# Folding rows h and -h ahead of the transform along h, and that transform in four 64x64 tiles of TensorE

## What is computed

```python
def afno_filter(x, w1, b1, w2, b2):
    xf = jnp.fft.rfft2(x, axes=(1, 2), norm='ortho')
    xf = xf.reshape(B, H, W // 2 + 1, NUM_BLOCKS, bs)
    xr, xi = (jnp.real(xf), jnp.imag(xf))
    o1r = relu(einsum(xr, w1[0]) - einsum(xi, w1[1]) + b1[0])
    o1i = relu(einsum(xi, w1[0]) + einsum(xr, w1[1]) + b1[1])
    o2r = einsum(o1r, w2[0]) - einsum(o1i, w2[1]) + b2[0]
    o2i = einsum(o1i, w2[0]) + einsum(o1r, w2[1]) + b2[1]
    yf = softshrink(o2r, LAM) + 1j * softshrink(o2i, LAM)
    return jnp.fft.irfft2(yf, s=(H, W), axes=(1, 2), norm='ortho') + x

h = layer_norm(x, n1_g, n1_b)
h = afno_filter(h, w1, b1, w2, b2) + x
residual = h
h = layer_norm(h, n2_g, n2_b)
h = gelu(h @ mw1 + mb1)
return h @ mw2 + mb2 + residual
```

## Time and profile before

| | us |
|---|---|
| median of 3 runs | 1629.3 (1629.04 to 1630.48) |
| the profiled execution, its own time | 1629.48 |
| its span, first to last instruction | 1627.7 |
| TensorE matmul busy | 1556.1 (96%) |
| VectorE busy | 990.3 (61%) |
| ScalarE busy | 889.3 (55%) |
| GpSimd busy | 620.4 (38%) |
| granted TensorE clock, mean | 1.000 |

### The profile page before, as it was taken

How to read it: one execution, slowest core, us unless ns; L and a number is a source line. 1 busy time by engine, 2 the same in 40 slices (tenths; PEclk the granted TensorE clock), 3 DMA queues, 4 the chain that set the end, 5 groups by cost and what they waited for, 6 DMA issues and landing times.

```text
span 1627.7 us, 43919 instructions
## 1 busy us (share of the span) xinstructions
PE 1556.1 (96%) x16132; PEld 1379.1 (85%) x16132; DVE 990.3 (61%) x2433; ACT 889.3 (55%) x1638; POOL 620.4 (38%) x782
## 2 busy tenths in 40 slices
PE   0999999999999899999999989999999989999999
PEld 0987888888998788888898888888889879888888
DVE  7967556656537665665655766565663675555553
ACT  5544366666534356666643436666662443666665
POOL 5800046776800017677660003667673000111111
PEclk9999999999999999999999999999999999999999
DMA  8410713333300062333420052333331006011111
GB/s 225 172 45 3 241 49 107 104 99 119 98 15 3 9 240 86 108 101 99 124 79 2 3 203 66 104 110 97 104 111 46 3 3 207 27 39 32 32 39 46
DMA packets 168583, 138.30 MB, mean 85 GB/s; under 512 B 10882, under 2 KB 132484, under 8 KB 168452
## 3 DMA queue, kind: packets, MB, share of 16 engines
q1 hardware_dynamic: 167268, 136.24, 26.6%
q10 hardware_dynamic: 1184, 0.20, 0.1%
HBM read 69.30 MB, written 67.11 MB: 84 GB/s over the span
## 4 chain that ended last, share of the span: by engine, by line
PE 93%; DVE 3%; ACT 1%; SPq 1%; DMA 1%; issue 1%; POOL 0%; ACTq 0%; DVEq 0%
PE ps L797 27%; PE ps L591 8%; PE ps L611 8%; PE ps L581 7%; PE ps L763 7%; PE ps L765 7%; PE ps L724 7%; PE ps L764 7%; PE ps L757 3%; PE ps L649 3%; PE ps L743 3%; PE ps L749 3%; SPq L431 1%; DMA first<-in_x_dram 1%; PE ps L779 1%
## 5 line engine op out<-in xcount | busy, mean ns | idle before, releaser
L797 PEld LDWEIGHTS ps<-mw,gel 128*128 128x128 f32 x4000 | 520.6, 191 | 42.3
L797 PE MATMUL ps<-mw,gel 128*128 128x128 f32 x4000 | 523.7, 274 | 0.0
L907 ACT ACTIVATE gel<-ps,mb1f 128x512 f32<-128x512 f32 x500 | 343.7, 687 | 250.6 <-PE ps L765 219.7
L1473 POOL TENSOR_TENSOR arena<-arena,mb2rep 128x512 f32<-128x512 f32 x125 | 160.2, 1282 | 634.5 <-ACT hn L893 634.5
L763 PE MATMUL ps<-hth,mw1h 128*128 128x512 f32 x512 | 259.7, 507 | 4.5 <-DVE vsb L1119 1.7
L1462 POOL TENSOR_SCALAR arena<-xnext,rstd,shift 128x128 f32<-128x128 f32 x360 | 159.4, 462 | 207.6 <-DVE shift L1356 207.6
L893 ACT ACTIVATE hn<-arena,shift,rstd 128x128 f32 (+1 forms) x512 | 221.6, 483 | 16.8 <-DVE shift L1356 16.8
L765 PE MATMUL ps<-hth,mw1l 128*128 128x512 f32 x512 | 202.1, 395 | 0.0
L764 PE MATMUL ps<-htl,mw1h 128*128 128x512 f32 x512 | 200.8, 392 | 0.0
L1203 DVE TENSOR_TENSOR arena<-ps,arena 128x512 f32 (+1 forms) x60 | 41.5, 691 | 252.0 <-PE ps L749 233.4
L871 ACT COPY gsb<-ps 128x512 f32<-128x512 f32 x128 | 69.1, 589 | 159.1 <-PE ps L611 153.0
(11 more groups left out here) (111 smaller groups left out, 2125.6 us busy)
## 6 DMA issues: line engine op xcount, KB each, us to landing
arena<-aside SPq DMA_DIRECT2D x128, 256.0 KB, 4.8
aside<-gz SPq DMA_DIRECT2D x96, 256.0 KB, 3.0
between<-xout SPq DMA_DIRECT2D x62, 256.0 KB, 2.3
out_dram<-xout SPq DMA_DIRECT2D x62, 256.0 KB, 2.3
xnext<-between SPq DMA_DIRECT2D x60, 256.0 KB, 3.0
aside<-first SPq DMA_DIRECT2D x32, 256.0 KB, 2.3
xnext<-in_x_dram SPq DMA_DIRECT2D x30, 256.0 KB, 3.1
first<-in_x_dram SPq DMA_DIRECT2D x1, 960.0 KB, 7.4
```

What stands on the lines that cost most here:

```text
L797: mm = pe.matmul(ps[:, r % 2, P * i:P * i + P], gel[:, r % 2, m, P * i:P * i + P], mw2[:, s // IMAGES, m, :], start=(m == 0 and i == 0), s ...
L907: act.activation(gel[:, r % 2, m, :], ps[:, 2 + m % 2], ACT.Gelu, bias=mb1f[:, s // IMAGES, m:m + 1]).then_inc(gelu_out, 1)
L1473: pool.tensor_tensor(t, t, b, ALU.add).then_inc(mb2_done, 1)
```

## The change

In steps 1 to 3 the rows of the image are laid out so that slots 64 to 127 hold the mirror rows (-h) of slots 0 to 63 in the same order (`zplace`; GpSimd and VectorE write the four rows of such a tile reversed).

dft_w becomes `mirrored`: each channel is done twice with 64 of the 128 slots as stationary operand, rows h into the even bank of a pair (sign 0) and rows -h into the odd bank (sign 1). Two channels, 64 partitions of output each, go to the two column halves of the array. A pair of banks (d, 16 of them) holds eight channels. ScalarE copies the bank of rows h to SBUF (`upper_copy`, into `hn`), then VectorE adds and subtracts the other bank (`fold_out`, two 128x512 operations) into the "folded" layout. TensorE waits for the folds of two pairs before (`evicted(s, 2 * d - 3)`).

dft_h then has 64 rows per product: sums with the even part (65 columns), differences with the sines and a correction (95 columns), for two halves of the array's rows. With both q together (`units=(0, 1)`) these are four 64x64 products on four different tiles. The two units of a pair are issued together, behind one wait for the copies of both, and signal together; units 0 and 1 at the start are issued singly, on two tiles. The frequencies along h are stored in another order (0, 64, evens, odds), with the same widths of the pieces in mix1 (65 and 63 columns). ih and idft_w take the lower half of the rows in the new order; `h2_odds` and `h2` read the reversed side on the subtraction instead of the addition. Step 0 stays as it was (`whole_dft_h`). The constants grow by 160 columns.

```diff
-CONSTS = 7 * P + MASKS
 EVEN = KWS + 1
+FOLD_E, FOLD_O = EVEN, P - EVEN + KWS // 2
+MASK_AT = 7 * P + FOLD_E + FOLD_O
+CONSTS = MASK_AT + MASKS
...
-    k_of = np.concatenate([k, -k[1:-1]])
+    ks = np.concatenate([[0, KWS], np.arange(2, KWS, 2), np.arange(1, KWS, 2)])
+    fh = np.concatenate([np.cos(turn * np.outer(h, ks)), np.sin(turn * np.outer(h, ks[2:]))], 1) * scale
+    k_of = np.concatenate([ks, -ks[2:]])
+    fold_e, fold_o = fh[:HALF, :EVEN].copy(), fh[:HALF, P - FOLD_O:].copy()
+    fold_e[-1] = scale * (ks % 2 == 0)
+    fold_o[:, :KWS // 2] = 0
+    fold_o[-1] = -scale * (np.arange(FOLD_O) < KWS // 2)
+    folds = np.tile(np.concatenate([fold_e, fold_o], 1), (2, 1))
     ih = np.concatenate([np.cos(turn * np.outer(k_of, h[:HALF + 1])),
                          np.sin(turn * np.outer(k_of, -h[HALF + 1:]))], 1) * scale
+    ih[:, HALF:] = ih[:, :HALF - 1:-1].copy()
     de = 2 * np.stack([cos, -sin], 2)[:, :KWS]
...
+        folded = [a.rearrange("p (k o a b d) -> p k o a b d", o=2, a=2, b=2, d=QUART) for a in flat]
...
+        def zplace(j, r):
+            return (2 * j + r // 2 + TILES // 2) * ROWS if r % 2 else tile_of(j, r) * ROWS
...
                 if s == 0:
                     pe.wait_ge(a_act, cg + 1)
-                elif cg % 2:
-                    pe.wait_ge(a_dve, CGROUPS // 2 * (s - 1) + cg // 2 + 1)
-                else:
-                    pe.wait_ge(a_act, CGROUPS + CGROUPS // 2 * (s - 1) + cg // 2 + 1)
+                else:
+                    pe.wait_ge(a_dve, CGROUPS * (s - 1) + cg + 1)
...
                 for cg in range(CGROUPS):
-                    if s and cg == 3:
-                        pe.wait_ge(lo_out, TILES * s)
+                    if s:
+                        mirrored(s, cg // 2, cg % 2)
+                        continue
                     if cg >= 4:
...
-            def dft_h(s, n):
+            def mirrored(s, d, sign):
+                if d == 1 and sign:
+                    pe.wait_ge(lo_out, TILES * s)
+                if d >= 2 and not sign:
+                    evicted(s, 2 * d - 3)
+                q, slots = d // 8, slice(HALF, H) if sign else slice(0, HALF)
+                for i in range(GROUP):
+                    for g in range(2):
+                        t = KWS // 2 * q + KWS // 4 * g + GROUP // 2 * (d % 8) + i // 2
+                        mm = pe.matmul(ps[HALF * g:HALF * g + HALF, 2 + 2 * (d % 2) + sign, P * i:P * i + P],
+                                       rows_of(s)[:, t, slots, i % 2], FW, start=(i == 0), stop=True,
+                                       skip_group_check=True)
+                mm.then_inc(s1_mm, 1)
+            def dft_h(s, n, units=(0,)):
+                if s:
+                    g = spectrum_of(n + units[-1])
+                    if g >= 2:
+                        pe.wait_ge(g_out, 2 * BATCHES * s + g - 1)
+                    for i in range(GROUP):
+                        for o in range(2):
+                            for u in units:
+                                q = (n + u) % 2
+                                for x in range(2):
+                                    own_rows = slice(HALF * x, HALF * x + HALF)
+                                    cols = slice(HALF * (x ^ q), HALF * (x ^ q) + HALF)
+                                    dst = slice(P * i, P * i + EVEN) if o == 0 else slice(P * (i + 1) - FOLD_O, P * (i + 1))
+                                    mm = pe.matmul(ps[cols, q, dst],
+                                                   folded_of(s)[own_rows, GROUP * (g // 2) + i, o, q].rearrange(
+                                                       "p r c -> p (r c)"),
+                                                   FOLDS[o][own_rows], start=(i == 0 and o == 0), stop=True,
+                                                   skip_group_check=True)
+                    mm.then_inc(s2_mm, len(units))
+                    return
+                for u in units:
+                    whole_dft_h(s, n + u)
+            def whole_dft_h(s, n):
...
                     quarters(j0, j1, depth, (0, EVEN), (0, EVEN), even, start)
-                    quarters(j0, j1, depth, (1, KWS), (EVEN, P), even)
-                    quarters(j0, j1, depth, (EVEN, P), (1, KWS), plus)
+                    quarters(j0, j1, depth, (2, EVEN), (EVEN, P), even)
+                    quarters(j0, j1, depth, (EVEN, P), (2, EVEN), plus)
                     return quarters(j0, j1, depth, (EVEN, P), (EVEN, P), minus)
...
                 pe.wait_ge(spec_done, 1 + s // IMAGES)
                 mix1(s, 0)
-                for q in range(2):
-                    dft_h(s, 4 + q)
+                dft_h(s, 4, (0, 1))
...
                     if p + 3 < PAIRED:
-                        for q in range(2):
-                            dft_h(s, 2 * p + 6 + q)
+                        dft_h(s, 2 * p + 6, (0, 1))
...
-                odd = v_of(s)[:, :, bass.ds(p * -ROWS + (H - ROWS), ROWS), :]
+                odd = v_of(s)[:, :, bass.ds(p * ROWS + HALF, ROWS), :]
...
+            def upper_copy(s, q, j, r):
+                act.wait_ge(s1_mm, CGROUPS * s + CGROUPS // 2 * q + 4 * j + 2 * r + 1)
+                act.copy(hn[:, r].rearrange("p a b -> p (a b)"), ps[:, 2 + 2 * r]).then_inc(a_act, 1)
...
-                    for g in range(2):
-                        with act.Fori(0, CGROUPS // 16) as j:
-                            for r in ((0, 2) if s else range(4)):
-                                a_out(s, q, g, j, r)
+                if s == 0:
+                    for q in range(2):
+                        for g in range(2):
+                            with act.Fori(0, CGROUPS // 16) as j:
+                                for r in range(4):
+                                    a_out(s, q, g, j, r)
+                else:
+                    for q in range(2):
+                        with act.Fori(0, CGROUPS // 8) as j:
+                            for r in range(2):
+                                upper_copy(s, q, j, r)
...
-            def a_out(s, q, g, j, r):
-                dve.wait_ge(s1_mm, CGROUPS * s + CGROUPS // 2 * q + CGROUPS // 4 * g + 4 * j + r + 1)
-                evict_a(dve.tensor_copy, s, q, g, 4 * j + r, r).then_inc(a_dve, 1)
+            def fold_out(s, q, j, r):
+                dve.wait_ge(a_act, CGROUPS + CGROUPS // 2 * (s - 1) + CGROUPS // 4 * q + 2 * j + r + 1)
+                dve.wait_ge(s1_mm, CGROUPS * s + CGROUPS // 2 * q + 4 * j + 2 * r + 2)
+                upper = hn[:, r].rearrange("p a b -> p (a b)").rearrange("p (i k r) -> p k r i", i=GROUP, r=2)
+                lower_ = ps[:, 3 + 2 * r].rearrange("p (i k r) -> p k r i", i=GROUP, r=2)
+                for o, op in enumerate((ALU.add, ALU.subtract)):
+                    dst = folded_of(s)[:, :, o, q, :, bass.ds(GROUP * (2 * j + r), GROUP)]
+                    dve.tensor_tensor(dst, upper, lower_, op).then_inc(a_dve, 1)
...
             def h2_odds(s, a, b):
                 top, low, _, odd = first_sums(s, a, b)
-                own.add(dve.tensor_tensor(top, odd[:, ::-1], top, ALU.add))
-                own.add(dve.tensor_tensor(low, low, odd, ALU.subtract))
+                own.add(dve.tensor_tensor(top, odd, top, ALU.add))
+                own.add(dve.tensor_tensor(low, low, odd[:, ::-1], ALU.subtract))
...
-                        for g in range(2):
-                            with dve.Fori(0, CGROUPS // 16) as j:
-                                for r in (1, 3):
-                                    a_out(s, q, g, j, r)
+                        with dve.Fori(0, CGROUPS // 8) as j:
+                            for r in range(2):
+                                fold_out(s, q, j, r)
...
-            def scale(s, h0, tmp):
-                pool.tensor_tensor(by_row(tmp), ztile(s, h0), gains(gain1[:, :]), ALU.mult).then_inc(gz_done, 1)
+            def scale(s, h0, tmp, mirror=False):
+                z = ztile(s, h0)[:, ::-1] if mirror else ztile(s, h0)
+                pool.tensor_tensor(by_row(tmp), z, gains(gain1[:, :]), ALU.mult).then_inc(gz_done, 1)
...
-                    h0 = ROWS * tile_of(j, r)
+                    h0 = zplace(j, r)
                     for k in range(ROWS):
                         row = (2 + r % 2) * ROWS + k
-                        ins = pool.tensor_scalar(zrow(s + 1, h0 + k), pairs(xnext[:, r, k, :]), rstd[:, r // 2, row:row + 1],
+                        ins = pool.tensor_scalar(zrow(s + 1, h0 + (ROWS - 1 - k if r % 2 else k)), pairs(xnext[:, r, k, :]), rstd[:, r // 2, row:row + 1],
```

More of the change, by code:

```diff
@@ L125, in dft_constants @@
     mask = (block[:, None] == np.arange(BLOCKS)[None]).astype(np.float64)
[L126 removed]
+    parts = [fw.reshape(P, P), fh, ih, de.reshape(P, P).T, do.reshape(P, P).T, np.eye(P), reverse, folds]
     sign = np.where(np.arange(P) % HALF < QUART, 1.0, -1.0)[:, None]
@@ L709, in first_pair @@
                 t = slice(GROUP // 2 * a, GROUP // 2 * b)
```

(6 more changed lines are left out.)

24 lines of the change are left out of this document (12 added, 12 removed).

## The result

The change made the kernel slower: 1648.9 us median of four runs (1645.1 to 1650.3) against 1629.2 (1629.0 to 1630.5), a ratio of 1.0115 with a 95% interval of 1.0097 to 1.0134. The forecast was 1615.3 with a range up to 1626, so it was wrong in sign and by 33.6 us.

A forecast was written before the change was run, and what follows sets the result against it. TensorE led the chain, but ScalarE's copies and relus were to decide the filter's new period. Three steps of -5.9 + 0.85 make -15.2, with +1.0 it is -14.2: from 1629.5 to 1615.3 us, range 1610 to 1626.

The forecast's parts named there:

- The evictions: In dft_w's loop, VectorE's fold pair takes 1.39 us, the loop 3.75 against TensorE's 3.77: cost 0.
- The tight-chain rival: A fold pair takes 1.85 us instead of 1.39 (time 1626), or dft_h 1.42 (1625 to 1626); chance 18%.
- the ring: In the filter, ScalarE's two copies and two relus between mix1 starts take 4.41 us, left as it is.
- steady period of 4.41: In the filter, the distance between mix1 starts falls from 4.79 to 4.41 us; 11 intervals give 4.2 a step.
- a lower granted clock: Listed sign of a wrong forecast: the granted clock falls in the filter, which now has gaps; no size given.
- dft_w: Half-width products run two at a time on the column halves, two costing what one full product did, 118 ns.
- the rival of 1705 us: In dft_w the column halves do not run side by side: +30.2 us a step, time about 1705; chance 8%.
- dft_h itself: In the filter, dft_h for two units falls from 1.98 to 1.14 us, with 1.42 kept for the range.
- two chains that I had both at 4.41: Behind a mix1: ScalarE's copies and relus, and the single wait for both copies ahead of dft_h; each 4.41 us.
- Behind dft_w: After dft_w, dft_h(1) starts 0.7 us later and takes 0.15 more, issued singly: loss 0.85 us a step.
- Step 2, scaling the weights: Scaling holds VectorE 1.5 us between the folds of bank pairs 7 and 8: loss 1.0 us, once.
- GpSimd and the MLP: Reversed rows written by GpSimd and VectorE cost nothing; the MLP keeps its work and limits.

The follow-up runs named there:

- the last version: Changed kernel with folds in order and idle products, half of mix2's products left out in steps 1 to 3, the rest 128 columns wide: 1610.1 us, ratio 0.9882.

## Why the prediction was wrong

The medians part the 33.6 us between forecast and result. From 1648.9 (changed kernel) folds in order bring 23.4, idle products 6.2, a fifth fewer instructions 9.2, and the end is 1610.1, 5.2 under the forecast. The parts are those of this order of adding. The last 9.2 was measured in a kernel that leaves half of mix2 out, and no kernel here that computes everything has it.

- **The evictions (the step that failed first).** I priced a fold pair at 1.39 us by rows of VectorE that read no SBUF operand with a stride; it was 2.06. The loop I had written down was TensorE 1.89 and 0.32, folds 1.39, 0.15 back, 3.75. In the trace its terms are 1.70 and 0.45 (first to last start of a pair's products, and from there to the fold), 2.06, and 0.06 back: 4.27, as the chain shows. So the mechanism was right and one term was mis-sized, by 0.67; I had called the chain one that just fits, at a cost of 0. Against the 3.77 that I had, the loop costs 0.25 for each of 16 pairs, and the last folds end 0.67 later: 4.7 a step, 14 in three, which is the first half of the ledger. The tight-chain rival was this very mechanism, even with its reason ("operands from SBUF and PSUM at once, with a stride"), but I had bounded it at 1.85 and given it 18%. The copy of L362 wrote the same places at 0.69 and lulled me: its strided side was in PSUM. No row showed a strided read from SBUF by VectorE, and the upper bound should have lain well beyond the nearest row.
- **dft_h and the filter, the ring.** Right in size where it ran clean: 4.38 to 4.46 in such pairs, 4.40 throughout where supply suffices; the interval with edges 4.95 to 5.01. In the last version the stretch from the first mix1 is 77.6 us against 84.0, -6.4 a step where I had -5.9. But the steady period of 4.41 that the sum used for 11 intervals a step was not kept: the late ones were 4.93 in the mean, 0.52 over it. Seven of them in each of three steps make 10.9 of the 15.9 us that the filter lacks, and two falls of the clock 3.2. What was missing was the price of issuing: I replaced 224 instructions per 4.79 us (47 a us) by 320 per 4.41 (73 a us) and named no limit for that. This is the second failed step, a term put at nothing, and none of my rivals had it.
- **The clock.** I named a lower granted clock as a sign that would prove me wrong but gave it no price. It fell, behind waits of TensorE, and cost about 1.6 us each time, about 5 us in the median. Idle products in those waits saved 6.2 and 8.1 us, by the clock and by something else.
- **dft_w.** The column halves do run side by side, as I took it: 110 ns a pair against 118 assumed. So the rival of 1705 us was rightly small, and there were 2 us a step to be had that the folds hid. Their loads hid under products on the same rows.
- **dft_h itself.** 1.13 us between starts for its 64 instructions, against 1.14. It starts 3.14 behind mix1 (I had 3.22) and its last instruction 4.25 behind it; the relus end at 4.28 and the next mix1 starts at 4.43. So of the two chains that I had both at 4.41 the ring of the relus decides, and the other is some 0.15 shorter. That I had them alike was no insight, the result does not depend on it.
- **Behind dft_w** I had +0.85 a step. With folds in order the whole stretch to mix1 is 31.85 against 33.06: dft_w 2.0 shorter, the tail 0.79 longer. Right.
- **Step 2, scaling the weights.** I had +1.0 for it. The stretch of step 2 is longer than that of step 1 by 0.2 before, by 2.0 after, and with folds in order still by 1.9 (33.77 against 31.85). So about 1.8 was lost, once: the place was right, the size too small by 0.8.
- **GpSimd and the MLP.** 620.4 and 618.8 us busy, and 275.85 against 275.84 for the rest of a step: unchanged, as said.

**Open.** Why do idle products shorten the late intervals as well, and by more than the clock explains? Why did 59 a us already fail in the kernel with halves of mix1, while 58 a us ran without a gap in the last version? A plain rate does not tell the two apart; I have shown that the count matters, not how it is fetched. Rolling the pairs into a loop on TensorE, which would take the supply away altogether as in the MLP (2 packets on q8 in 100 us there), was not tried.

The best version that computes everything is the one with folds in order and idle products: 1619.3 us, 0.7% under the kernel before and 1.8% under the change as it was made.

## What to carry to other kernels

Splitting products into smaller tiles leaves the columns alone and multiplies instructions: count instructions a us before and after, not only passes, wherever the code is unrolled. Price an elementwise operation by a row with the same memory, direction and stride for each operand; where no row has that stride in SBUF, the upper bound lies far above the contiguous one, and ScalarE's copy out of PSUM can do the reordering for nothing. A chain of waits that fits by hundredths is not a zero but a coin toss, and its waits can cost the clock besides. Count the columns of weight loads as well as those that products move.

## What the runs showed of the hardware

- VectorE, two operands of 128x512, one in SBUF and one in PSUM: 684 ns with SBUF in order, 1065 to 1070 when one SBUF operand, read or written, goes 4 bytes at a time. A stride of 512 bytes on the PSUM operand cost nothing, and ScalarE scattered into SBUF from PSUM at 587 ns.
- TensorE was fed about 65 instructions a us in unrolled code (320 per 4.93 us, 416 per 6.4 us), with gaps that no semaphore explains beyond that. Demands of 58 and below (the last version, the kernel before) ran without gaps, one of 59 with some. Queue q8 shows it coming: 13 packets in the 50 us from 500 to 550 against 9 before and 10 in the last version, and 24 packets more in the whole program for 6228 instructions more, 260 to a packet.
- Two 128x64 tiles on the two column halves run side by side, loads included: 110 ns for the two, for 128 columns, though both use all rows. Two 64x128 tiles on the two row halves do as well (starts 6 to 8 ns apart), but a pair took 112 ns for 64 columns, while four tiles of 64x64 took 58. The loads have 128 columns there, and loads of that width come at 111 ns at best in the kernel before; that they set the time is not shown by a run of its own.
